# Softmax exponentials in two halves, and no filler matmuls between the input tiles

## The reference

```python
y = softmax(where(causal, (q @ k.T) * scale, min)) @ v      # layer 0, q = x @ wq
x = layernorm(x + y @ wo)
for c in range(6):
    q = ew[c, 0] * (nodes[in_q] @ We[eq] + be[eq])
    k = ew[c, 1] * (nodes[in_k] @ We[ek] + be[ek])
    v = ew[c, 2] * (nodes[in_v] @ We[ev] + be[ev])
    o = mha(q, k, v, Wq[c], Wk[c], Wv[c], Wo[c])             # 8 heads, no mask
    nodes[c] = act_w[c] * o + q
out = layernorm(x + layernorm_g_b(nodes[5]))
```

## Time and profile before

| what | us |
|---|---|
| median of 2 runs | 7925.72 (7921.73 to 7929.72) |
| the profiled execution, its own time | 7691.81 |
| its span, slowest core (core 4) | 7690.7 |
| spans of the 8 cores | 7666.1 to 7690.7 |
| mean granted TensorE clock of the cores | 0.855 to 0.858 |
| busy: TensorE, ScalarE, VectorE | 5626.2, 2452.9, 1746.5 |

### The profile page before, as it was taken

How to read it: one execution, slowest core, us unless ns; L and a number is a source line. 1 busy time by engine, 2 the same in 40 slices (tenths; PEclk the granted TensorE clock), 3 DMA queues, 4 the chain that set the end, 5 groups by cost and what they waited for, 6 DMA issues and landing times.

```text
span 7690.7 us, 67599 instructions; the slowest of 8 cores (7666.1 to 7690.7 us)
## 1 busy us (share of the span) xinstructions
PE 5626.2 (73%) x21918; PEld 2142.4 (28%) x22346; DVE 1746.5 (23%) x2473; ACT 2452.9 (32%) x2040; POOL 59.1 (1%) x71
## 2 busy tenths in 40 slices
PE   7455658777796778977778967789777789656654
PEld 3112123222342223432223422224222234212211
DVE  3432222111213112141112231111411112332233
ACT  1123302444223443214441134432144421324422
POOL 0000000000000000000000000000000000000000
PEclk9668878899897999978989978999888899778777
DMA  3001031000320011320003300023200024000000
GB/s 83 11 28 28 17 93 34 11 17 11 71 55 17 12 22 39 86 46 17 12 11 82 78 17 11 16 45 77 55 17 11 11 60 99 6 26 10 20 28 22
DMA packets 179543, 271.78 MB, mean 35 GB/s; under 512 B 5696, under 2 KB 116608, under 8 KB 179222
## 3 DMA queue, kind: packets, MB, share of 16 engines
q0 software_dynamic: 69680, 111.42, 8.5%
q10 hardware_dynamic: 96128, 113.25, 4.7%
q1 hardware_dynamic: 13414, 42.76, 1.6%
HBM read 286.55 MB, written 67.11 MB: 46 GB/s over the span
## 4 chain that ended last, share of the span: by engine, by line
PE 54%; ACT 21%; DVE 11%; issue 9%; DMA 4%; DVEq 1%; ACTq 0%; SPq 0%; POOLq 0%
PE psS L57 27%; PE psA L57 20%; ACT Dm L57 16%; ACT rowb L57 4%; PE psY L57 4%; PE psM L57 3%; DVE LNw L57 3%; DVE Dm L57 3%; DVE rowb L57 3%; DVE psS L57 1%; DMA x1w<-x 1%; DVE mask_sb L57 1%; DVE x1w L57 1%; DMA nsc<-x1w 1%; DMA A<-nsc 1%
## 5 line engine op out<-in xcount | busy, mean ns | idle before, releaser
L57 ACT ACTIVATE Dm<-psS,negC 128x2048 bf16<-128x2048 f32 x848 | 1668.0, 1967 | 2112.2 <-PE psS L57 1921.8
L57 PE MATMUL psS<-A,B 128*128 128x512 bf16 x3282 | 946.2, 410 | 413.4 <-ACT Dm L57 383.0
L57 DVE CAST mask_sb<-rowb 1x512 bf16<-1x512 f32 x192 | 79.7, 415 | 2938.8 <-ACT rowb L57 2938.8
L57 PE MATMUL psA<-Dm,Wb 128*128 128x512 bf16 (+1 forms) x2565 | 645.8, 405 | 94.7 <-DVE Dm L57 82.5
L57 PE MATMUL psY<-Dm,Cv 128*128 128x512 bf16 x1651 | 503.3, 431 | 273.1 <-DVE Dm L57 224.9
L57 PE MATMUL psA<-Dm,Cv 128*128 128x512 bf16 x1654 | 481.5, 415 | 269.4 <-DVE Dm L57 223.0
L57 PE MATMUL psM<-Dm,on_b 128*1 128x512 bf16 x1808 | 544.5, 421 | 163.9 <-ACT Dm L57 156.7
L57 PEld LDWEIGHTS psS<-A,B 128*128 128x128 bf16 x3392 | 323.6, 100 | 1047.5 <-issue 912.1
L57 PE MATMUL psS<-Dm,Wb 128*128 128x512 bf16 (+1 forms) x2561 | 588.8, 379 | 3.3
L57 PE MATMUL psA<-Dm,on_b 128*1 128x512 bf16 (+1 forms) x1712 | 492.8, 413 | 11.9 <-DVE Dm L57 8.0
L57 DVE TENSOR_SCALAR Dm<-psA,be_fm 128x512 bf16<-128x512 f32 x240 | 180.3, 751 | 978.6 <-PE psA L57 939.9
(11 more groups left out here) (117 smaller groups left out, 3693.3 us busy)
## 6 DMA issues: line engine op xcount, KB each, us to landing
A<-nsc ACTq DMA_DIRECT2D x36, 1024.0 KB, 12.1
Wb<-ffn_We POOLq DMA_DIRECT2D x15, 2048.0 KB, 13.5
qsp<-Dm SPq DMA_DIRECT2D x6, 4096.0 KB, 23.6
Dm<-qsp ACTq DMA_DIRECT2D x24, 1024.0 KB, 6.4
nsc<-x1w POOLq DMA_DIRECT2D x20, 1024.0 KB, 11.2
x1w<-x ACTq DMA_DIRECT2D x32, 512.0 KB, 3.7
B<-x1b ACTq DMA_DIRECT2D x16, 1024.0 KB, 21.5
Wb<-ffn_Wv POOLq DMA_DIRECT2D x6, 2048.0 KB, 18.3
```

The lines of the kernel that those rows point to most:

```text
L57: r = f(*a, **k)
```

## The change

First, in `attn_unit`, the exponential of a group is issued as two, over banks 2 and 3 and over banks 4 and 5. The first half waits for the second score matmul of the group, the second half for the fourth; in the masked group of a causal unit both wait for VectorE's mask adds. Banks 2 and 3 come free with the first half. In `emit_pv_quad` the first two value matmuls wait for the first half, the other two for the second; the four sum matmuls follow. Second, in the input loading, six matmuls for each tile, whose result nobody reads, are taken out.

```diff
@@ -522,22 +522,34 @@
                 else:
+                    gPE.wait(SE, pev - 2)
+                SE.activation(out=Dp[:, g4 * 4:g4 * 4 + 2, :].rearrange("p a b -> p (a b)"),
+                              in_=psS[:, 0:1024], func=AF.Exp,
+                              bias=negC[:, negC_col:negC_col + 1], scale=1.0)
+                m0 = gSE.n
+                if not (causal and g4 == qb):
                     gPE.wait(SE, pev)
-                SE.activation(out=Dp[:, g4 * 4:g4 * 4 + 4, :].rearrange("p a b -> p (a b)"),
-                              in_=psS[:, 0:2048], func=AF.Exp,
+                SE.activation(out=Dp[:, g4 * 4 + 2:g4 * 4 + 4, :].rearrange("p a b -> p (a b)"),
+                              in_=psS[:, 1024:2048], func=AF.Exp,
                               bias=negC[:, negC_col:negC_col + 1], scale=1.0)
-                exp_marks.append(gSE.n)
-                for j in range(4):
-                    bank_free[2 + j] = (gSE, gSE.n)
+                exp_marks.append((m0, gSE.n))
+                bank_free[2] = bank_free[3] = (gSE, m0)
+                bank_free[4] = bank_free[5] = (gSE, gSE.n)
...
             def emit_pv_quad(g4):
-                gSE.wait(TE, exp_marks[g4])
+                m0, m1 = exp_marks[g4]
+                gSE.wait(TE, m0)
                 if g4 == 0:
                     bfree(ybank, TE)
                     bfree(mbank, TE)
-                for j in range(4):
+                for j in range(2):
+                    kt = g4 * 4 + j
+                    TE.matmul(out=psY_u, lhsT=vh_fn(kt), rhs=Dp[:, kt, :],
+                              start=(kt == 0), stop=(kt == n_kt - 1))
+                gSE.wait(TE, m1)
+                for j in range(2, 4):
@@ -674,11 +686,6 @@
             dX[sl].n += 16
-            if tt == 0:
-                bfree(2, TE)
-            for _ in range(6):
-                TE.matmul(out=psS[:, 0:512], lhsT=on_b[:], rhs=mask_sb[:, 0, :],
-                          start=True, stop=True)
             dX[sl].wait(TE)
```

## The result

The changed kernel is faster. Its median over 11 runs is 7525.85 us (7402.36 to 7767.41), against 7780.67 (7692.02 to 7939.14, 10 runs) for the kernel before measured with it. Some executions of either kernel take some per cent longer, with one die or both at a lower mean clock, and the ratio of 0.963 (interval 0.957 to 0.969) is that of the others; the medians have a ratio of 0.967. The forecast was 7603 against 7925.7, a ratio of 0.959. The profiled executions compare best, since both show the clock levels 1.0 and 0.5 only: 7691.8 before, 7403.0 after, 288.8 less where 323 were forecast.

What follows compares the result with a forecast made beforehand. No engine was taken to bound the whole kernel: TensorE and ScalarE take turns. Node blocks -317, causal stage -15 and removed warm-up matmuls +9 gave -323 us, from 7925.7 to 7603, range 7475 to 7750.

Steps and rivals of the forecast that it cites:

- A half exponential costs 1.11: ScalarE's 128x1024 exponential: 1.11 us, on the line through the 128x512 (0.69) and 128x2048 (1.97) costs.
- rival 3: ScalarE in plain steps: half exponential has a large fixed cost, up to 1.97 us; kernel slower, 8215 us; chance 0.04.
- rival 4: Node blocks: half near 1.0 us and rarer clock drops, 17 us gained a block, about 7490; chance 0.12 with beyond.
- A plain step of 2.68: One score group to the next without a boundary: 2.68 us instead of 3.29, a gain of 0.61.
- (a): Unit with a boundary, from scores 0 to the first PV matmul: 7.11 us for 7.20.
- (b): Unit with a boundary, from the first PV matmul to scores 3: 6.24 us for 6.76.
- (c): Unit with a boundary, from scores 3 to the next unit's scores 0: 2.68 us for 3.29.
- 13.2 a block: Gain per node block: 11.0 us by steps plus 2.2 from the clock; 24 blocks give 317.
- 15 in the causal stage: 80 causal exponentials: 15 us gained, between 0 and 35; 32 masked ones at about nothing, 48 others up to 0.61 each.
- 9 for the filler: Input loading without the warm-up matmuls: 9 us lost, between 0 and 20; 7 in transposes, rest at first projection.
- Rival 1: Unit boundary: longer idle brings a second low-clock stretch, 1.7 us a unit, 326 in all; time unchanged, about 7925; chance 0.09.
- Rival 2: TensorE's clock falls under denser steps, gain only 0.1 us a step, 72 in all, about 7845; chance 0.05.

Runs made afterwards that it cites:

- Experiment 2: Changed kernel with the matmuls that sum the exponentials using all 128 columns of ones; 7749.5 us at first, lowest 7404.5 in the repeat, ratio 0.962 to the kernel before.
- experiment 5: Changed kernel with whole exponentials again in layer 0's 32 masked groups; causal blocks sum to 544 us, against 538 in the changed kernel.
- experiment 1: Changed kernel with the six matmuls per input tile put back; spans 7381 to 7404 us on cores 0 to 3.
- experiment 4: The changed kernel measured again without any edit, to watch the granted clock; 7416 to 7680 us.
- Experiment 3: Older unit's finish issued ahead of younger unit's tail: on the changed kernel 6943 to 7282 us; on the kernel before, spans 7175 to 7199 (cores 0 to 3).
- experiment 7: Changed kernel with older unit's finish issued earlier, row's Ln and Exp issued later, and sums over 128 columns; lowest time 6843 us, ratio 0.889 to the kernel before.

## Why the prediction was right, and where it was off

The direction, the mechanism and the range held: 7525.9 lies within 7475 to 7750, 77 below the forecast. That it lies there is in part luck, since the range was set from the first median of the kernel before, 7925.7, and this kernel's median over 10 runs was 7780.7. The forecast gain of 323 from there would give 7458, below the range; the medians differ by 255. The comparison that carries is that of the profiled executions: the gain was 289 where the sum had 323. By its steps:

- *A half exponential costs 1.11.* 1.114. The line through two lengths was good to 1%, and rival 3 (a large fixed cost) fell, and with it rival 4's half near 1.0.
- *A plain step of 2.68.* It took 2.79. The mis-sized term is TensorE's own work: 12 x 0.2157 came from a projection, where all weights have one shape. Experiment 2 shows 2.59 with uniform weights. The timeline of before had it one row further than the earlier trace rows quote it: the value matmuls start at 2444.89 and the sums 0.95 later, where four equal matmuls take 0.86:

```profile
2445.84 1.02 PE L57 MATMUL psM<-Dm,on_b 128*1 128x512 bf16 x4
```

- *The boundary, (a) 7.11, (b) 6.24, (c) 2.68.* Measured 7.31, 6.29 and 2.79 in the unit above (2383.44, 2390.75, 2397.04, 2399.83): 16.39 for 16.03. In (a) the Ln begins 3.35 after scores 0 instead of the 3.14 forecast: it is no longer the exponential that it waits for but the last sum matmul. That one is late because the third of scores 0 waits for the second half of the group before (1.38 for 1.04 in the row at 2383.44), and because of the slower steps. The idle came to about 3, as forecast, and is still ended by the context multiply.
- *13.2 a block.* 11.4, in sum 262 + 12 = 275 for 317. The clock term was good: the time at 0.5 in a node block fell by 5.1, worth 2.5 where 2.2 were taken. The mis-sized term is the 11.0 by steps, of which 8.9 came. The unit shown above took 16.39 for 16.03, and six such units make the 2.1. The windows show 0.94 in the shorter blocks and 0.88 to 0.90 in the longest.
- *15 in the causal stage.* 5.6, with 2.6 at the starts 8.2. The size was within its bounds, but the reason was wrong: the masked groups, put at nothing, gave all of it (experiment 5), and the unmasked ones nothing. Why these gave nothing was not tested by itself.
- *9 for the filler.* 4.8, of which putting the filler back returned 4.1 (experiment 1). The transposes did take 1.94 at the low level, but little of it was passed on: the first projection matmul comes 3.2 later (78.9 for 75.7 as means of the cores) where the sum had 7. The rest was probably taken up by the idle on the transfer, which was not tested by itself. By the 32nd projection matmul 4.9 are lost, so that the low start of the projection cost 1.7 where about 2 were taken.
- *No term.* The 10.5 us that the stretches between the blocks gained stand in no term of the sum. Without them the gain would have been 278.
- *Rival 1, a second stretch at the low clock:* none; less time at 0.5, not more. Its price was also set on 192 units where only 144 have such a boundary (144 x 1.7 = 245). Its mechanism showed elsewhere: in experiment 2 the denser steps of the node blocks lost all they gained to the clock, with the idle left in place.
- *Rival 2, the clock gives way.* The level exists. It is not the change alone that brings it: a kernel without the halves shows it too (experiment 4). Whether it becomes more frequent with denser work stays open; the runs are too few.

The remark that the gained time on scores 1 is lost at the boundary was the important one. Experiment 3 shows that the order on VectorE, a finished unit's copy behind an unfinished unit's cast, was worth more than the halves: 19 us a block against 11.4.

## What to carry to other kernels

Splitting an operation that frees a buffer lets two engines overlap, and pays until the other engine's own work is the step; take that work from rows with the same mix of weights and lengths, not from a uniform stretch. Then look for the idle that is left: here a queue order (a short chain of a younger unit ahead of an older unit's last two instructions) cost more than the step, and at TensorE it cost the clock as well. The halves paid with and without that idle (10.9 and about 9.5 a block), but the smaller gain of the wide sums vanished in the node blocks as long as it was there; so take the idle out first.

## What was not expected of the hardware

- **Alternating weights.** Four matmuls of 512 columns take 0.86 us among equals. Where groups of four with 128-column weights and groups with one column alternate, a group takes 0.95 when the next one has the other width: the value matmuls and the sums do (2366.34, 2367.30, 2368.25 above). With the sums widened, which widens their output from one row to 128 as well, all take 0.86 to 0.87.
- **A third clock level.** The profile of before shows 1.0 and 0.5 only, and so do four others. In the first run of experiment 2 dense stretches stood at 0.81. Core 0, one window of 100 us:

```profile
3100.00:3200.00 100.00, 91.70 (x343) 37.36 (x342) 24.04 (x32) 6.83 (x11) 1.76 (x2) 0.79 0.48 118
```

  It lasted 1794 to 2365 us on each core of that run and 0 to 1807 in others, often on one die alone. The two first runs of the kernel before, 234 us above its profile, are as long as one of a later series (7917.5) that has a mean clock of 0.816 to 0.818 on one die; their own clocks are not on record, so that this level explains the distance is likely and not shown. The level is the 13/16 that the Trainium skill names, page "TensorE: Matmul & The Clock Gate", section "Seeing it yourself". But the page has it come on once three cores of a die run dense matmuls and stay while the load lasts, and five of the twelve profiles do not show it on any core, though TensorE is busy for 103 to 104 of 104 us on all eight cores in the window 1160 to 1264 of the kernel before.
- **The clock can take back density.** Shorter steps with the same idle behind them gave 244 us more at 0.5 in the node blocks and no shorter node block (experiment 2). The same edit without the idle gave 8 us more at 0.5 and 48 us of span (experiment 7).
